# Experts with the gate on each expert's output, and another order of work in the selective scan and the last attention

## The chip, the cores and the metric

The kernel runs on one core of a Trainium2 chip. A core has TensorE (PE, matrix products into PSUM), VectorE (DVE), ScalarE (ACT), GpSimd (POOL) and SyncE (SP), which runs no arithmetic here. Each engine works through its own list of instructions in order, and they wait for one another by semaphores. The metric is the device time of the whole program in microseconds. The numbers of the text are microseconds where no unit stands.

## The reference, cut to what matters

Eight sublayers on 2048 tokens of 128 features, each followed by an addition and a LayerNorm. The change touches the second (`L0_ffn`), the fifth (`L2_attn`) and the seventh (`L3_attn`), and the LayerNorm behind them.

```python
x = layernorm(x + L0_ffn(x))     # and so on for the eight sublayers

def L0_ffn(x):                   # 8 experts, hidden 512, the best 2 of each token count
    logits = x @ router_w.T + router_b
    topk_val, topk_idx = top_k(logits, 2)
    weights = softmax(topk_val)
    outs = [silu(x @ w1a.T + b1a) * (x @ w1b.T + b1b) @ w2.T + b2 for each expert]
    return sum over the two chosen of outs[idx] * weight

def L2_attn(x):
    xs, z = split(x @ W_in)      # 128 channels each; both: silu(depthwise conv, 4 taps)
    dt_low, Bc, Cc = split(xs @ W_xdbl)        # 64, 16, 16
    delta = softplus(dt_low @ W_dt + 2 * inv_dt)
    # for each of 16 states n and each token l of 4 sequences of 256:
    h = exp(-(n + 1) * delta) * h + delta * xs * Bc[n]
    y = sum over n of h * Cc[n]  + xs * D
    return concat(y, silu(z)) @ W_out + b_out

def L3_attn(x):                  # 16 heads, 4 key/value heads of 64
    return softmax(q @ k.T) @ v @ o_w.T + o_b
```

## The kernel before, in words

Features or channels lie on the 128 partitions and tokens along the free axis in *blocks* of 512 (4 blocks, 16 *tiles* of 128 tokens). For LayerNorm the tokens lie on the partitions (`X`, 16 tiles). Each sublayer is a class with one method for each engine (`pe`, `act`, `dve`, `pool`) that issues that engine's instructions in program order; a counter such as `hid` or `gated` is a semaphore, and `e.wait_ge(*self.hid(j))` waits for its j-th step. There is no planner: the order written in these methods is the order of the work. No DMA stands in the loops that the change touches.

*Experts* (`Experts`, line 585). The loop has 128 jobs i: block b = i // 32, expert x = i // 4 % 8, and one quarter kb = i % 4 of the hidden features. For a job, PE does six f16 matmuls of 512 columns (`first`: the operands are split into a high and a low f16 part, L680 to L682) into two banks; ACT takes silu of the first bank into `S1` (L770); POOL multiplies it by the gate row of the expert, spread over the partitions, `GS` (L881); DVE adds the bias to the second bank and multiplies (L820, into `HF`, the gated product); ACT rounds that to f16 (L776); DVE takes the remainder, the low part (L814); PE does three down matmuls (L723 to L725), three jobs behind. All 32 jobs of a block add up in one bank (6 or 7), which begins with the gated second bias (`MB2` by the gates `GT`). `GS` is made by PE (L709, a spread of the gates by a constant matrix) and ACT at the first job of each expert. On DVE the order within an iteration is: low part of job i−2, gated product of job i−1, and up to iteration 24 a pair of instructions for the low parts of the next weights (`w_low`, L801). At the end of a block ACT copies the bank to SBUF, PE transposes it (L730) and DVE does the LayerNorm's addition and statistics (L305, L312, L315) before it goes on with the next product. The scaling of all 16 tiles follows after the last block. Before the loop, DVE picks the experts and computes the gates (`gates`), and PE and ACT transpose and copy them.

*Selective scan* (`Mamba`, line 1295). 32 *units* u: a half of the tokens (1024, two blocks b = 0, 1) by 16 states n. For a unit PE spreads the row B for both blocks (`rows_b`, L1460) and the row C for both (`rows_c`, L1468, both into bank 6, so the second waits for ACT's copy of the first, L1595) and adds up the unit before (`add_up`, two fp32 matmuls, L1478). ACT makes the decay of unit u + 2 (`decay_of`, L1588). DVE scales the input (`scale_in`, two instructions), and does the scan (`dve_scan`, L1689). POOL multiplies the result by the C row (L1718). Parts 2 and 3 of the projections, the delta of the second half and the second convolution (`pe_gate`) are distributed over units 1 to 31 by the `if u ==` chains in `pe`, `act`, `dve` and `pool`. `dve_y` (L1694) finishes the first half's output.

*Last attention* (`Attention`, line 2314). 32 pairs ji, each of 16 groups g: PE's scores, DVE's row maxima (L2743), with which PE continues (L2497), ACT's exponentials (L2638), sums on DVE (L2761) and POOL (L2813). After every eighth pair DVE adds the block (`dve_add`, g = 7 of ji % 8 = 0), and in the pair behind takes the statistics (g = `STATS` = 0) and the scale factors with the scaling of 4 tiles (g = `SCALE` = 2); ACT scales the other half of these tiles. `LayerNorm(k, 1)` scales block by block; `LayerNorm(k)` scales once, after all four.

## Time and profile before

| | |
|---|---|
| time, median of 3 runs | 2797.37 (2792.01 to 2798.61) |
| the profiled execution's own time | 2786.94 |
| its span | 2784.8 |
| mean granted TensorE clock (share of full speed) | 0.959 |
| PE, DVE, ACT, POOL busy (page) | 88%, 73%, 52%, 43% |

The busy shares are means over eleven stages that follow one another. The times in the timelines count from the span's start. In them, several like instructions in a row are put together (x2), and "[0.76 <-ACT WK L776]" says that the engine had been idle for 0.76 us and that ACT's instruction of line 776 ended this. Experts' first layers (L680) start from 110 to 418, the scans (L1689) from 675 to 813, and the last attention's row maxima (L2743) from 1407 to 2582.

### The profile page before, as it was taken

The numbers are of one execution on the slowest core, as the hardware profiler recorded it, in microseconds if no ns is written. First come the engines' busy times: TensorE is split into PE (matmuls) and PEld (weight loads), VectorE is DVE, ScalarE is ACT, GpSimd is POOL, SyncE is SP. The second block draws the span as 40 slices with busy tenths as digits, with TensorE's granted clock in tenths as the row PEclk, the third lists the DMA queues.
The fourth block names the chain that finished last, engine by engine and source line by source line (L and its number), as shares of the span: only waits on it lengthen the run. The fifth ranks groups of instructions, "written<-read, shape, count | busy, mean of one in ns | idle before, by whom it ended". The sixth has DMA issues, their size and how long they took to land.

```text
span 2784.8 us, 40142 instructions
## 1 busy us (share of the span) xinstructions
PE 2443.4 (88%) x14918; PEld 1121.1 (40%) x14918; DVE 2040.9 (73%) x3152; ACT 1440.9 (52%) x2509; POOL 1185.3 (43%) x748
## 2 busy tenths in 40 slices
PE   6689995797777987798679999999999999999897
PEld 4434332444234665466423333333333333333344
DVE  7686666616888984897578888788878888788542
ACT  5465552534646773576235555455545555455462
POOL 1155550402645541554105555445545555455530
PEclk9799997898998999999889999999999999999999
DMA  5000000101000000000010000000000000000000
GB/s 205 1 1 1 1 1 0 54 1 42 1 1 16 1 1 1 1 1 2 16 42 5 9 9 9 9 7 7 9 9 9 9 9 9 5 9 9 9 1 16
DMA packets 20831, 37.92 MB, mean 14 GB/s; under 512 B 10462, under 2 KB 12638, under 8 KB 19612
## 3 DMA queue, kind: packets, MB, share of 16 engines
q1 hardware_dynamic: 20636, 35.35, 3.7%
q8 instruction: 119, 1.95, 0.3%
q14 instruction: 76, 0.62, 0.1%
HBM read 32.99 MB, written 2.35 MB: 13 GB/s over the span
## 4 chain that ended last, share of the span: by engine, by line
PE 56%; DVE 30%; issue 7%; ACT 5%; POOL 1%; DMA 0%; ACTq 0%; DVEq 0%; POOLq 0%; SPq 0%
PE PS L2536 12%; PE PS L2527 12%; PE PS L1184 6%; DVE NR L2743 5%; PE PS L2497 5%; DVE W L2761 2%; DVE WK L820 2%; DVE NR L270 2%; DVE WK L2075 2%; PE PS L1478 2%; PE PS L1166 2%; DVE WK L2051 2%; DVE WK L267 1%; ACT WK L776 1%; PE PS L2483 1%
## 5 line engine op out<-in xcount | busy, mean ns | idle before, releaser
L2743 DVE TENSOR_REDUCE NR<-PS 128x2 f32<-128x1024 f32 x512 | 626.1, 1223 | 208.5 <-PE PS L2498 208.4
L2638 ACT ACTIVATE WK<-PS 128x1024 f32<-128x1024 f32 x512 | 496.9, 1022 | 488.9 <-PE PS L2527 416.5
L2813 POOL TENSOR_TENSOR W<-W,WK 128x1024 f32<-128x1024 f32 x224 | 527.2, 2354 | 482.0 <-DVE W L2761 413.0
L2536 PE MATMUL PS<-WK,W 128*64 128x512 f32 x2048 | 494.1, 603 | 0.0
L2527 PE MATMUL PS<-WK 64*128 64x512 f16 (+1 forms) x4096 | 485.5, 377 | 0.0
L2761 DVE TENSOR_TENSOR W<-W,WK 128x1024 f32<-128x1024 f32 x224 | 284.9, 1272 | 14.4 <-ACT WK L2638 14.3
L2527 PEld LDWEIGHTS PS<-WK 64*128 64x128 f16 (+1 forms) x4096 | 199.3, 94 | 220.1 <-ACT WK L2638 6.5
L881 POOL TENSOR_TENSOR WK<-WK 128x512 f32<-128x512 f32 x128 | 168.0, 1313 | 154.0 <-ACT WK L770 154.0
L2497 PE MATMUL PS<-WK 64*128 64x512 f16 x512 | 196.4, 384 | 36.9 <-DVE NR L2743 34.7
L2536 PEld LDWEIGHTS PS<-WK,W 128*64 128x64 f32 x2048 | 124.1, 136 | 249.3 <-issue 174.3
L2498 PE MATMUL PS<-WK 64*128 64x512 f16 x512 | 196.4, 384 | 0.0
L1184 PE MATMUL PS<-WK,W 128*128 128x512 f16 x768 | 166.1, 379 | 0.0
L2497 PEld LDWEIGHTS PS<-WK 64*128 64x128 f16 x512 | 47.8, 93 | 285.9 <-DVE NR L2743 227.7
L814 DVE TENSOR_TENSOR WK<-WK 128x512 f16<-128x512 f32 x128 | 96.9, 757 | 77.0 <-ACT WK L776 77.0
L2098 POOL TENSOR_TENSOR WK<-WK 128x512 f32<-128x512 f32 x64 | 113.4, 1793 | 93.9 <-DVE WK L2035 93.7
L1988 ACT ACTIVATE WK<-PS,WK 128x192 f32<-128x192 f32 (+1 forms) x256 | 103.7, 428 | 89.8 <-DVE WK L2075 89.7
L776 ACT ACTIVATE WK<-WK 128x512 f16<-128x512 f32 x128 | 80.6, 630 | 107.9 <-DVE WK L820 107.8
L2106 POOL TENSOR_TENSOR WK<-WK 128x768 f32<-128x768 f32 (+1 forms) x64 | 91.5, 1448 | 101.9 <-DVE WK L2028 101.9
L1184 PEld LDWEIGHTS PS<-WK,W 128*128 128x128 f16 x768 | 75.1, 98 | 90.6
L820 DVE SCALAR_TENSOR_TENSOR WK<-PS,WK 128x512 f32<-128x512 f32 x128 | 95.0, 742 | 8.9 <-POOL WK L881 8.9
L680 PE MATMUL PS<-WK 128*128 128x512 f16 x256 | 99.5, 389 | 1.6 <-ACT WK L770 1.6
L1718 POOL TENSOR_TENSOR WK<-WK 128x512 f32<-128x512 f32 x64 | 80.0, 1271 | 47.4 <-ACT WK L1595 42.2
(364 smaller groups left out, 4343.4 us busy)
## 6 DMA issues: line engine op xcount, KB each, us to landing
XB<-l_rdens SPq DMA_DIRECT2D x62, 128.0 KB, 2.9
W<-in_mw SPq DMA_DIRECT2D x8, 512.0 KB, 12.2
W<-in_l2w SPq DMA_DIRECT2D x1, 3114.0 KB, 12.2
W<-in_f1w SPq DMA_DIRECT2D x1, 2816.0 KB, 18.7
W<-in_l3w SPq DMA_DIRECT2D x1, 2816.0 KB, 10.3
W<-in_f3w SPq DMA_DIRECT2D x1, 2816.0 KB, 9.8
W<-in_mw SPq DMA_DIRECT2D x8, 256.0 KB, 12.2
CBB<-in_cbb SPq DMA_DIRECT2D x1, 1360.0 KB, 8.3
```

The source lines that it names most:

```text
L820: e.scalar_tensor_tensor(out=self.HF[j % 3], in0=k.bank(2 + j % 3), scalar=self.MB1[:, x * 8 + 4 + kb:x * 8 + 5 + kb], in1=self.S1[j % 3], ...
L881: e.tensor_tensor(s1, s1, self.GS[i // 4 % 2], ALU.mult).then_inc(self.gated.sem)
L1184: i = e.matmul(k.bank(2 + (n + 2) % 6), wp[p][:, kb, o], src[q][:, kb, s_], start=kb == 0 and j == 0, stop=kb == 3 and j == 2)
L2098: e.tensor_tensor(p5[:, :, :, hf, :], q5[:, :, :, 1 - hf, :], self.SN[:, t, :, hf * 32:hf * 32 + 32].unsqueeze(2).broadcast_to([P, 2, 8, 3 ...
L2497: e.matmul(k.bank(6), q[0:64, ts_], self.KH[0:64, g, ks], start=True, stop=True)
L2498: e.matmul(k.bank(7), q[64:128, ts_], self.KH[64:128, g, ks], start=True, stop=True).then_inc(self.maxs.sem)
L2527: m = e.matmul(k.bank(2 * (kt % 2) + i), keys[own, :], queries[own, :], start=j == 0, stop=j == 3)
L2536: m = e.matmul(k.PS[64 * i:64 * i + 64, 4, :], self.V[:, kt, g, :], self.PTB[kt // 2 % 2][:, kt % 2, i, :], start=kt == 0, stop=kt == NT - 1)
L2638: e.activation(self.PTB[kt // 2 % 2][:, kt % 2, :, :], self.k.PS[:, 2 * (kt % 2):2 * (kt % 2) + 2, :], ACT.Exp, scale=1.0 / 64).then_inc(s ...
L2743: e.tensor_reduce(self.PM[ji % 2][:, u // 4, :, u % 4], self.k.PS[:, 6:8, :], AX.X, ALU.max).then_inc(self.maxes.sem)
L2761: e.tensor_tensor(ac, ac, p, ALU.add).then_inc(self.acc0.sem)
L2813: e.tensor_tensor(ac, ac, p, ALU.add).then_inc(self.acc1.sem)
```

## The change

*Experts.* silu is no longer multiplied by the gate. DVE's product writes in place into `S1` (four buffers instead of three), the low part is a scalar_tensor_tensor that scales by 0.125, and each expert has a bank of its own, 6 + n % 2 with n the number of block and expert. When an expert's four down products are in, DVE multiplies the bank by the gate row into `TM` (the first expert of a block: into the sum `ACC`), and POOL adds `TM` to `ACC`. The second bias is added in `pe_rows`, where PE multiplies by the gates `GT` and turns the sum, seven jobs after the block's end; `dve_rows` does addition and statistics at iterations 41, 73, 105 and at the end. The gate's spread is now at the third job of each expert; the transposes of the gates (`pe_gates`, `act_gates`) are inside the loop at i = 2, and four parts of the low weights stand around `gates`.

*Scan.* Adding up half 0 of the unit before is put between the two C rows. The pieces for parts 2 and 3 move by a unit or more on PE and ACT, and `dve_y` from unit 16 to 17.

*Last attention.* The statistics are taken in two halves at g = 4 of the two pairs behind a block; the scaling is done once, after the last block, for 16 tiles.

The diff, cut to its core:

```diff
-    def dve_stats(self, e, b):
-        k = self.k
+    def dve_stats(self, e, b, part=0, parts=1):
+
+        k, n = self.k, 4 // parts
         xs = k.X[:, 4 * b:4 * b + 4, :]
         e.wait_ge(*self.added(b + 1))
-        for j in range(4):
+        for j in range(n * part, n * part + n):
             e.bn_stats(k.ST[:, b, j, :], xs[:, j, :]).then_inc(self.stats.sem)
-        e.wait_ge(*self.stats(8 * b + 4))
-        for j in range(4):
+        e.wait_ge(*self.stats(8 * b + 2 * n * part + n))
+        for j in range(n * part, n * part + n):
             e.bn_aggr(k.MV[:, b, j, :], k.ST[:, b, j, :]).then_inc(self.stats.sem)
...
-        self.S1 = [wk(16384 + i * 512, 512) for i in range(3)]
-        self.HF = [wk(17920 + i * 512, 512) for i in range(3)]
...
+        self.S1 = [wk(16384 + i * 512, 512) for i in range(4)]
+        self.HP = [wk(18432 + i * 512, 512).bitcast(F16).rearrange("p (s n) -> p s n", s=2) for i in range(4)]
+        self.TM = wk(20480, 512)
+        self.ACC = [k.XB[:, :, :].rearrange("p t f -> p (t f)"), wk(20992, 512)]
+        self.MB1 = wk(21504, 64)
...
+        for i in range(128 + 3):
+            if i < 128:
+                b, x, kb = self.job(i)
+                if kb == 2:
+                    if i == 2:
+                        self.pe_gates(e)
+                    else:
+                        e.wait_ge(*self.gs(i // 4))
+                    if x == 2 and b:
+                        e.wait_ge(*self.ln.added(b))
+                    e.matmul(k.bank(5), k.cb("selm", x * 128, (x + 1) * 128, p1=96), self.G3[0:96, b * 512:(b + 1) * 512], start=True, stop=True).then_inc(self.gbc.sem)
+                if i > 1:
+                    first(i)
+                if x == 1 and kb == 3 and b:
+                    self.pe_rows(e, b - 1)
+            if i >= 3:
+                b, x, kb = self.job(i - 3)
+                n = (i - 3) // 4
+                hb, acc = self.HP[(i - 3) % 4], k.bank(6 + n % 2)
+                q = slice(1024 + kb * 128, 1024 + (kb + 1) * 128)
+                if not kb and n >= 2:
+                    e.wait_ge(*self.gated(n - 1))
+                if n < 2 and not kb:
+                    e.wait_ge(*self.gt(8))
+                e.wait_ge(*self.hl(i - 2))
+                e.matmul(acc, self.WH[x][:, q], hb[:, 0, :], start=not kb, stop=False)
+                e.matmul(acc, self.WL[x][:, q], hb[:, 0, :], start=False, stop=False)
+                e.matmul(acc, self.WH[x][:, q], hb[:, 1, :], start=False, stop=kb == 3).then_inc(self.down.sem)
+        self.pe_rows(e, 3)
...
+    def pe_rows(self, e, b):
+
+        k, PS = self.k, self.k.PS
+        e.wait_ge(*self.gs(8 * b + 10 if b < 3 else 32))
+        e.wait_ge(*self.summed(7 * b + 7))
+        for j in range(4):
+            o, t = PS[:, 5, j * 128:(j + 1) * 128], 4 * b + j
+            e.matmul(o, self.GT[0:8, t * 128:(t + 1) * 128], k.c("mb2", p1=8), start=True, stop=False)
+            i = e.matmul(o, self.ACC[b % 2][:, j * 128:(j + 1) * 128], k.eye, start=False, stop=True)
+        i.then_inc(self.otr.sem)
...
-                if x == 7 and kb == 3:
-                    e.wait_ge(*self.gs(8 * (b + 1) + (b < 3)))
-                    e.wait_ge(*self.out(b + 1))
-                    for q in range(4):
-                        i_ = e.transpose(PS[:, 5, q * 128:(q + 1) * 128], k.XB[:, q, :], k.eye)
-                    i_.then_inc(self.otr.sem)
...
+        for i in range(128 + 1):
+            if i == 2:
+                self.act_gates(e)
+            if i < 128:
+                b, x, kb = self.job(i)
+                if kb == 3:
+                    n = i // 4
+                    if n >= 2:
+                        e.wait_ge(*self.gated(n - 1))
+                    e.wait_ge(*self.gbc(n + 1))
+                    e.activation(self.GS[n % 2], k.bank(5), ACT.Copy, scale=1.0 / 64).then_inc(self.gs.sem)
+                if i >= 4:
+                    e.wait_ge(*self.hl(i - 3))
+                e.wait_ge(*self.up(2 * i + 1))
+                e.activation(self.S1[i % 4], k.bank(i % 2), ACT.Silu, bias=c("mb1", x * 8 + kb, x * 8 + kb + 1), scale=1.0 / 64).then_inc(self.silu.sem)
+            if 1 <= i:
+                j = i - 1
+                if j >= 4:
+                    e.wait_ge(*self.down(j - 3))
+                e.wait_ge(*self.hid(j + 1))
+                e.activation(self.HP[j % 4][:, 0, :], self.S1[j % 4], ACT.Copy, scale=0.125).then_inc(self.hh.sem)
...
-                    e.activation(k.XB[:, :, :].rearrange("p t f -> p (t f)"), k.bank(6 + b % 2), ACT.Copy, scale=1.0 / 512).then_inc(self.out.sem)
-                    self.ln.act(e, b)
...
-        e.tensor_scalar(self.MB2[0:8, :], c("mb2", p1=8), 512.0, None, ALU.mult).then_inc(self.bias.sem)
+        w_low(1, 0)
+        w_low(1, 1)
         self.gates(e)
-        for n in range(4, 4 + self.AHEAD):
-            w_low(n // 4, n % 4)
-        for i in range(128 + 3):
+        w_low(1, 2)
+        w_low(1, 3)
+        e.wait_ge(*self.bias(1))
+        for i in range(128 + 4):
             if 2 <= i < 130:
                 j = i - 2
                 hb = self.HP[j % 4]
                 e.wait_ge(*self.hh(j + 1))
-                e.tensor_tensor(hb[:, 1, :], self.HF[j % 3], hb[:, 0, :], ALU.subtract).then_inc(self.hl.sem)
+                e.scalar_tensor_tensor(out=hb[:, 1, :], in0=self.S1[j % 4], scalar=0.125, in1=hb[:, 0, :], op0=ALU.mult, op1=ALU.subtract).then_inc(self.hl.sem)
             if 1 <= i < 129:
                 j = i - 1
                 b, x, kb = self.job(j)
                 e.wait_ge(*self.up(2 * j + 2))
-                e.wait_ge(*self.gated(j + 1))
-                e.scalar_tensor_tensor(out=self.HF[j % 3], in0=k.bank(2 + j % 3), scalar=self.MB1[:, x * 8 + 4 + kb:x * 8 + 5 + kb], in1=self.S1[j % 3], op0=ALU.add, op1=ALU.mult).then_inc(self.hid.sem)
+                e.wait_ge(*self.silu(j + 1))
+                e.scalar_tensor_tensor(out=self.S1[j % 4], in0=k.bank(2 + j % 3), scalar=self.MB1[:, x * 8 + 4 + kb:x * 8 + 5 + kb], in1=self.S1[j % 4], op0=ALU.add, op1=ALU.mult).then_inc(self.hid.sem)
...
+            if i >= 7 and i % 4 == 3:
+                self.dve_gate(e, i // 4 - 1)
+            if i > 32 and i % 32 == 9:
+                self.dve_rows(e, i // 32 - 1)
+        self.dve_rows(e, 3)
+
+    def dve_gate(self, e, n):
+
+        b, x = n // 8, n % 8
+        if not x:
+            if b >= 2:
+                e.wait_ge(*self.otr(b - 1))
+        elif n > 1:
+            e.wait_ge(*self.summed(7 * b + x - 1))
+        e.wait_ge(*self.gs(n + 1))
+        e.wait_ge(*self.down(4 * n + 4))
+        e.tensor_tensor(self.TM if x else self.ACC[b % 2], self.k.bank(6 + n % 2), self.GS[n % 2], ALU.mult).then_inc(self.gated.sem)
+
+    def dve_rows(self, e, b):
+        e.wait_ge(*self.otr(b + 1))
+        self.ln.dve(e, b, four(self.k.PS[:, 5, :]))
...
-        for i in range(128):
-            s1 = self.S1[i % 3]
-            if i % 4 == 0:
-                e.wait_ge(*self.gs(i // 4 + 1))
-            e.wait_ge(*self.silu(i + 1))
-            e.tensor_tensor(s1, s1, self.GS[i // 4 % 2], ALU.mult).then_inc(self.gated.sem)
+        for n in range(32):
+            b, x = n // 8, n % 8
+            if x:
+                acc = self.ACC[b % 2]
+                if x > 1:
+                    e.wait_ge(*self.summed(7 * b + x - 1))
+                e.wait_ge(*self.gated(n + 1))
+                e.tensor_tensor(acc, acc, self.TM, ALU.add).then_inc(self.summed.sem)
...
                 self.rows_b(e, u + 1, 0)
                 self.rows_b(e, u + 1, 1)
             self.rows_c(e, u, 0)
+            if u:
+                self.add_up(e, u - 1, 0)
             self.rows_c(e, u, 1)
             if u:
-                self.add_up(e, u - 1, 0)
                 self.add_up(e, u - 1, 1)
             if u == 1:
                 self.pe_low(e, 2)
-            elif u == 3:
+            elif u == 4:
                 self.pe_low(e, 3)
-            elif u == 5:
+            elif u == 6:
                 self.pe_dt(e, 2)
-            elif u == 7:
+            elif u == 8:
                 self.pe_dt(e, 3)
             elif self.Z0 <= u < self.Z0 + 16:
                 self.pe_gate(e, u - self.Z0)
...
             if u == 2:
                 self.act_low(e, 2)
             elif u == 4:
+                self.act_mid(e, 2)
+            elif u == 5:
                 self.act_low(e, 3)
-            elif u == 5:
-                self.act_mid(e, 2)
             elif u == 6:
+                self.act_mid(e, 3)
+            elif u == 7:
                 self.act_abs(e, 2)
                 self.act_pos(e, 2)
-            elif u == 7:
-                self.act_mid(e, 3)
-            elif u == 8:
+            elif u == 9:
                 self.act_abs(e, 3)
                 self.act_pos(e, 3)
-            elif u == 9:
+            elif u == 10:
                 self.act_exp(e, 1)
-            elif u == 10:
+            elif u == 11:
                 self.act_ln(e, 2)
                 self.act_ln(e, 3)
             elif u >= self.Z0 + 4 and (u - self.Z0) % 4 == 0 and u <= self.Z0 + 16:
...
                 self.dve_rem(e, 2)
             elif u == 5:
                 self.dve_rem(e, 3)
-            elif u == 16:
+            elif u == 17:
                 self.dve_y(e, 0)
                 self.dve_y(e, 1)
         e.wait_ge(*self.biased(1))
...
     PROJECT, AHEAD = 4, 5
     TOP, ROW, LOW = 4, 6, 6
     SUM, INVERT, MULTIPLY, PRODUCT = 1, 3, 4, 7
-    STATS, SCALE = 0, 2
+    STATS = 4
 
     def __init__(self, k, ld, const, rows):
         self.k, self.ld, self.const = k, ld, const
...
         self.rwide = k.counter("l3_reciprocals_wide", 31 * 32)
         self.ot = k.counter("l3_divided", 32)
         self.prod = k.counter("l3_products", 4)
-        self.ln = LayerNorm(k, 1)
+        self.ln = LayerNorm(k)
 
 
 
...
                     self.act_output(e, ji - 1)
                 if g == self.SUM and ji:
                     self.act_denominators(e, ji - 1)
-                if g == self.SCALE + 1 and ji > 8 and ji % 8 == 1:
-                    self.ln.act(e, ji // 8 - 1)
         self.act_output(e, 31)
         self.ln.act(e, 3)
 
...
                 if g == self.PRODUCT and ji and ji % 8 == 0:
                     e.wait_ge(*self.prod(ji // 8))
                     self.ln.dve_add(e, ji // 8 - 1, four(k.PS[:, 5, :]))
-                if g == self.STATS and ji > 8 and ji % 8 == 1:
-                    self.ln.dve_stats(e, ji // 8 - 1)
-                if g == self.SCALE and ji > 8 and ji % 8 == 1:
-                    self.ln.dve_scale(e, ji // 8 - 1)
+                if g == self.STATS and ji > 8 and 1 <= ji % 8 <= 2:
+                    self.ln.dve_stats(e, ji // 8 - 1, ji % 8 - 1, 2)
         self.dve_sum(e, 31, 7)
         self.dve_join(e, 31)
         self.dve_last_invert(e)
```

## Rows read from the trace of the kernel before

**Rows 1.** The page: busy time of each engine, and the chain that ended last.
```profile
PE 2443.4 (88%) x14918; PEld 1121.1 (40%) x14918; DVE 2040.9 (73%) x3152; ACT 1440.9 (52%) x2509; POOL 1185.3 (43%) x748
...
PE 56%; DVE 30%; issue 7%; ACT 5%; POOL 1%; DMA 0%; ACTq 0%; DVEq 0%; POOLq 0%; SPq 0%
```

**Rows 2.** Timeline, Experts loop: start us, us, engine line op [idle before <-releaser].
```profile
302.12 0.74 DVE L820 SCALAR_TENSOR_TENSOR WK<-PS,WK 128x512 f32<-128x512 f32 x1
303.62 0.69 DVE L814 TENSOR_TENSOR WK<-WK 128x512 f16<-128x512 f32 x1 [0.76 <-ACT WK L776]
304.22 0.75 DVE L820 SCALAR_TENSOR_TENSOR WK<-PS,WK 128x512 f32<-128x512 f32 x1
...
306.08 0.68 ACT L770 ACTIVATE WK<-PS,CB 128x512 f32<-128x512 f32 x1
...
306.90 1.27 POOL L881 TENSOR_TENSOR WK<-WK 128x512 f32<-128x512 f32 x1 [1.39 <-ACT WK L770]
...
307.83 0.88 DVE L814 TENSOR_TENSOR WK<-WK 128x512 f16<-128x512 f32 x1 [0.76 <-ACT WK L776]
...
308.78 0.39 PE L723 MATMUL PS<-WK 128*128 128x512 f16 x1 [0.19 <-DVE WK L814]
```

**Rows 3.** Timelines of DVE and PE, start and end of Experts.
```profile
133.96 0.74 DVE L820 SCALAR_TENSOR_TENSOR WK<-PS,WK 128x512 f32<-128x512 f32 x1
...
422.71 0.74 DVE L820 SCALAR_TENSOR_TENSOR WK<-PS,WK 128x512 f32<-128x512 f32 x1
...
427.13 1.09 PE L730 MATMUL PS<-CB,XB 128*128 128x128 f32 x4 [0.78 <-ACT XB L786]
```

**Rows 4.** Timelines of DVE and POOL, where both start close together.
```profile
146.83 1.70 DVE L801 SCALAR_TENSOR_TENSOR WK<-W,WK 128x256 f16<-128x256 f32 x2
147.11 1.27 POOL L881 TENSOR_TENSOR WK<-WK 128x512 f32<-128x512 f32 x1 [1.95 <-ACT WK L770]
...
156.82 0.61 DVE L801 SCALAR_TENSOR_TENSOR WK<-W,WK 128x256 f16<-128x256 f32 x2
157.11 1.44 POOL L881 TENSOR_TENSOR WK<-WK 128x512 f32<-128x512 f32 x1 [1.97 <-ACT WK L770]
...
2584.85 2.35 POOL L2813 TENSOR_TENSOR W<-W,WK 128x1024 f32<-128x1024 f32 x1 [1.16 <-DVE W L2761]
2584.87 3.40 DVE L2761 TENSOR_TENSOR W<-W,WK 128x1024 f32<-128x1024 f32 x1
```

**Rows 5.** Timeline of DVE, the end of block 0 of Experts.
```profile
208.36 0.74 DVE L820 SCALAR_TENSOR_TENSOR WK<-PS,WK 128x512 f32<-128x512 f32 x1
...
211.58 0.69 DVE L305 TENSOR_TENSOR X<-PS,X 128x512 f32<-128x512 f32 x1 [2.48 <-PE PS L730]
...
214.09 0.74 DVE L820 SCALAR_TENSOR_TENSOR WK<-PS,WK 128x512 f32<-128x512 f32 x1
```

**Rows 6.** One line's view, the scans: min/median/max ns, first and last start us.
```profile
L1689 DVE TENSOR_TENSOR_SCAN WK<-WK,PS x16: 2286/2287/2289, 675.2 to 744.0; 128x1024 f32<-128x1024 f32 x16
...
L1689 DVE TENSOR_TENSOR_SCAN WK<-WK,NR,PS x16: 2347/2347/2349, 748.4 to 812.8; 128x1024 f32<-128x1024 f32 x16
```

**Rows 7.** Timelines of PE and DVE in the scan.
```profile
720.48 0.60 PE L1460 MATMUL PS<-WK,CBB 96*128 96x512 bf16 x2
...
722.05 0.39 PE L1468 MATMUL PS<-WK,CBB 96*128 96x512 bf16 x1 [0.76 <-ACT WK L1595]
...
724.86 0.60 PE L1460 MATMUL PS<-WK,CBB 96*128 96x512 bf16 x2
...
753.70 1.61 DVE L1694 SCALAR_TENSOR_TENSOR WK<-WK,CB,PS 128x512 f32<-128x512 f32 x2 [2.92 <-PE PS L1478]
```

**Rows 8.** Timelines of DVE and PE in the last attention.
```profile
1798.24 0.16 DVE L323 TENSOR_SCALAR NR<-MV 128x4 f32<-128x4 f32 x1
...
1801.21 1.22 DVE L2761 TENSOR_TENSOR W<-W,WK 128x1024 f32<-128x1024 f32 x1
...
1803.62 0.39 PE L2497 MATMUL PS<-WK 64*128 64x512 f16 x1 [2.75 <-DVE NR L2743]
```

More of the change, by code:

```diff
@@ L751, in act, with act_gates @@
         e.activation(self.GW[:, 1, :], self.GW[:, 0, :], ACT.Exp).then_inc(self.gexp.sem)
+        for i in range(128 + 1):
[19 more added lines that the diff above has]
+                e.activation(self.HP[j % 4][:, 0, :], self.S1[j % 4], ACT.Copy, scale=0.125).then_inc(self.hh.sem)
+            n = i + 4 + self.AHEAD
+            if n < 32:
+                w_high(n // 4, n % 4)
+        for b in range(NB):
+            self.ln.act(e, b)
+    def act_gates(self, e):
+        k = self.k
         for b in range(NB):
@@ L757, in act @@
             e.activation(self.G3[0:96, s_], k.bank(7, p1=96), ACT.Copy).then_inc(self.gt.sem)
-        for i in range(128 + 3):
-            if i < 128:
-                b, x, kb = self.job(i)
-                if not kb:
-                    n = i // 4
-                    if n >= 2:
-                        e.wait_ge(*self.gated(4 * (n - 1)))
-                    e.wait_ge(*self.gbc(n + 1))
-                    e.activation(self.GS[n % 2], k.bank(5), ACT.Copy).then_inc(self.gs.sem)
-                if i >= 3:
-                    e.wait_ge(*self.hid(i - 2))
-                e.wait_ge(*self.up(2 * i + 1))
-                e.activation(self.S1[i % 3], k.bank(i % 2), ACT.Silu, bias=c("mb1", x * 8 + kb, x * 8 + kb + 1), scale=1.0 / 64).then_inc(self.silu.sem)
-            if 1 <= i < 129:
-                j = i - 1
-                if j >= 4:
-                    e.wait_ge(*self.down(j - 3))
-                e.wait_ge(*self.hid(j + 1))
-                e.activation(self.HP[j % 4][:, 0, :], self.HF[j % 3], ACT.Copy).then_inc(self.hh.sem)
-            n = i + 4 + self.AHEAD
-            if n < 32:
-                w_high(n // 4, n % 4)
-            if i >= 3:
-                b, x, kb = self.job(i - 3)
-                if x == 7 and kb == 3:
-                    e.wait_ge(*self.down(32 * (b + 1)))
-                    if b:
-                        e.wait_ge(*self.otr(b))
-                    e.activation(k.XB[:, :, :].rearrange("p t f -> p (t f)"), k.bank(6 + b % 2), ACT.Copy, scale=1.0 / 512).then_inc(self.out.sem)
-                    self.ln.act(e, b)
     def dve(self, e):
@@ L823, in dve @@
                 w_low(n // 4, n % 4)
-            if i >= 3:
-                b, x, kb = self.job(i - 3)
-                if x == 7 and kb == 3:
-                    e.wait_ge(*self.otr(b + 1))
-                    self.ln.dve(e, b, four(PS[:, 5, :]))
+            if i >= 7 and i % 4 == 3:
[16 more added lines that the diff above has]
+        self.ln.dve(e, b, four(self.k.PS[:, 5, :]))
     def gates(self, e):
```

52 lines of the change are left out of this document (11 added, 41 removed).

## The prediction

> **What bounds the kernel now.** I read the page first. TensorE (PE) is busy 88% of the span and has 56% of the chain that ended last, but DVE has 30% of it [rows 1], so the limit changes from stage to stage, and I went on stage by stage with the timelines.
>
> In the Experts loop the order on DVE is: low part of job j, gated product of job j+1, and so on. The product (L820) starts at 302.12; ACT rounds it; the low part (L814) starts at 303.62, after 0.76 of idle time that ACT's L776 ended; the next product starts at 304.22 [rows 2]. This is a ring, DVE to ACT to DVE, of 2.10 to 2.11 us for a job, and PE needs less: nine matmuls at 0.216 from start to start are 1.94, with a quarter of the gate's spread 2.0, and it does idle for DVE's low part (0.19 before 308.78 [rows 2]). GpSimd (POOL), busy 1.27 in every job, is not in the ring except at each expert's first job: its multiply starts late (306.90), and the low part takes 0.88 in place of 0.69 [rows 2]. 308.71 (its end) is 0.54 after POOL's end at 308.17: the low part did not run slower, it waited. So four jobs take 8.63 (4 times 2.11 and 0.19).
>
> In the scan (u = 0 to 31), DVE alone would need 1.29 for two input scalings, less an overlap, and 2.29 or 2.35 for the scan itself, 3.72 or 3.81 a unit; the starts of the 32 scans go from 675.2 to 812.8 [rows 6], 137.6 for 31 intervals, where DVE alone needs about 119. The rest is PE. Its cycle in the units with a gate convolution is 4.37 (720.48 to 724.86) [rows 7], and 0.76 of it is a wait for ACT's copy between the two C rows. In the last attention, PE and DVE hand the row maxima to and fro, and a stretch of other work on DVE stops PE: during the 2.97 from 1798.24 to 1801.21 and after it PE sat idle for 2.75 [rows 8].
>
> **The change, part by part.**
>
> *Experts, ring.* POOL's 128 multiplies of 1.27 go. The low part becomes a scalar_tensor_tensor with the same shapes; I take 0.69 (the types are the same, and the ring's other operand is unchanged). The rounding on ACT keeps its size, so the ring stays 2.11. Added on DVE: 32 products of bank and gate, PSUM against SBUF, 128x512; the LayerNorm's addition has that shape and took 0.69 [rows 5]. It is put right after a gated product, in the 0.76 in which DVE idles, so it costs nothing there. In the first block the slot also holds the low weights (a pair takes 0.61 undisturbed [rows 4]); five gates fall there, about 0.3 each, and four POOL additions delay the next pair by 0.2 each: 2.4.
>
> *Experts, POOL's 28 additions.* This is the term that decides. Each reads two SBUF operands, 1.27 as the multiplies of that shape, and starts when the gate product ends. A gate product starts 0.66 after the gated product L820, ends 0.60 after that one's end, thus at about 1.35; POOL starts 0.14 after what it waits for in the two-signal form (ACT's end 306.76 to 306.90 [rows 2]): 1.49. The low part starts at 1.50. A tie within 0.02. The loser waits for the winner's whole instruction: if POOL wins, the low part ends 0.54 after POOL, at 3.30 and not at 2.19, 1.06 to 1.1 later, in the ring; if DVE wins, POOL waits and nobody minds. Nearest rows: DVE starting 0.02 after POOL lost (3.40 for an instruction of 1.22 [rows 4]). Two pairs of DVE instructions, whose second starts 0.33 after the first: with POOL 0.28 behind the first it lost (1.70 for the pair), with POOL 0.29 behind it won (0.61, POOL 1.44) [rows 4]. So there DVE still wins when it starts about 0.04 after POOL; an instruction that starts from idle needs some 0.015 more, which puts the edge near 0.025, just where the lost case lies. I expect the low part 0.01 after POOL, so DVE wins, by a hair. Bounds: 0 and 1.06 for each of the 23 additions that lie in the ring outside the low weights' time. Three of them (second expert of blocks 1 to 3) wait for one signal only, so POOL is earlier and wins: 3.2. I take the other 20 at 0.
>
> The Trainium skill ("SBUF — State Buffer", the section on the engine ports) says that VectorE with two SBUF inputs and GpSimd share a port pair under an exclusive lock, and that whichever starts first has it for the whole instruction while the other fully blocks. The blocking agrees with the trace (0.88, 3.40). By its "starts first", POOL would win all 23; that is the first rival below. The pair of 0.61 shows a later start that won.
>
> *Experts, block ends.* Before: from product to product 5.73 (208.36 to 214.09) in place of 2.11, of which 2.48 is the wait for PE's transposes [rows 5]; 3.62 too much, three times. After: PE turns the sums four to seven jobs later. It waits for the gate row that ACT copies, does eight fp32 matmuls of 128 columns (about 2.1 at the slower clock, as the four transposes took 1.09 [rows 3]), and its next first layer is late for ACT by about 2.1, of which the ring feels 1.1; then DVE's addition and statistics, 1.93, stand where 0.76 was idle, 1.1 more. 2.2, and 2.7 with PE at the lower clock in part. From the third gated product (133.96) to the last (422.71) the kernel took 288.75 [rows 3]. After: 125 rings of 2.11 are 263.75, and 2.4, 3.2 and 8.1 make 277.4: minus 11.3.
>
> *Experts, ends.* The gates' transposes and copies (about 5.3) now come after the first gated product, not before it, and silu's table is loaded while DVE picks the experts. I place the third product at 129.6, not 133.96 [rows 3]: minus 4 (3 to 5). At the end, after the last down matmul: gate product 0.69, POOL 1.27, eight matmuls, where there were a copy of 0.6 and four transposes: plus 2.4 where the transposes end, at 428.22 [rows 3]. Experts: minus 12.9.
>
> *Scan.* Adding up half 0 before the second C row puts 0.86 of matmuls into the 0.76 wait. PE's cycle becomes 3.5 with the convolution, under DVE's 3.81. The old excess over DVE alone: 0.55 to 0.6 in each of eight units, 4.6; PE's backlog at units 6 and 8 1.3; the log's two table loads, after which a decay on ACT is late for DVE, and the backlog behind, 5.1; the outputs of the first half, 2.92 until PE's additions [rows 7], now a unit later when they are done; the start, 3.5, of which the new order takes 1.7. Sum 15.6, and half a microsecond behind the last scan. The remainders for channel part 3 are now taken by ACT and DVE in the same unit: DVE waits about 1.0. I forecast minus 14 (8 to 16), as some table-load stall may remain.
>
> *Last attention.* Three scale chains leave DVE: 2.97 each, 2.85 of it felt [rows 8]: minus 8.6. The statistics go from one 1.2 in group 0 to twice 0.6 in group 4, where DVE idles for PE's row matmuls but PE waits for the next maximum: plus 0.3, three times. The last scaling covers 16 tiles, not 4: ACT does eight of 0.4 in place of two, less transposes that follow behind: plus 1.8 (up to 2.3). Sum minus 5.9.
>
> Total: 12.9, 14 and 5.9 are 32.8. From the profiled execution's 2786.94, that gives 2754.1; the median of the three runs is 2797.37, 0.37% above it, so 2764.5, say **2765 us**.
>
> **The rivals.**
>
> *POOL wins every tie.* For: it is the plain order of starts, and the 0.02 case. Against: the pair at 0.61. Price 20 times 1.06, 21.2 more: 2786. A mixture lies between.
>
> *The scan gains half.* The table loads stall DVE as before and the late remainders cost more; with DVE winning the ties, 7 less: 2772.
>
> *PE stops in the new place (slower).* Half 0's addition stands before the second C row and so before ACT's copy and POOL's next product. If POOL's product of half 0 is not ready when PE gets there (it has about 0.4 to spare by my count), PE, ACT and POOL wait in a chain. From 0.4 of lateness on it decides; at one product's 1.27 a unit, less 0.4, 31 units lose 27 and the scan's 14 are gone: 2765 + 41, about 2806. Against: POOL idles a third of the unit.
>
> *The late transposes do not shorten the Experts* (block ends as before, plus the longer end): 2765 + 3: it stays in the first case's range.
>
> **How the numbers follow.** DVE wins 0.50 (own range 2756 to 2775); POOL wins 0.28; scan gains half 0.10; small mishaps of both kinds 0.08; PE stops 0.04. About 0.3% (8 us) is what a measurement of this kernel tells from no change. Faster by more than it is below 2789: nearly all of the first and third cases and four fifths of the second, whose 2786 lies 3 under that limit: 0.88 with half of the mishaps. Same 0.08, slower 0.04. The range reaches to the POOL case: 2753 to 2791.
>
> **What would show it.** In the profile after: the low part (128x512, f16 out) near 0.69 in each job, and 1.7 to 1.8 in three or in 23 of them, says who wins; product to product 2.11 between. Gate products must not be ended by a wait for PE. Block ends near 4.8, not 5.73. The scans' starts should span about 123, without 4.37 intervals; a wait of DVE for ACT's remainder of about 1.0 appears once. In the last attention no PE gap of 2.75. The prediction is wrong if the ring's period is not 2.11, if low parts wait elsewhere, or if scan intervals stay above 3.9.

## The result

The changed kernel is slower by 0.3%: 2803.72 (median of 16 runs, 2794.98 to 2806.08) against 2793.49 before (16 runs, 2788.43 to 2798.61), ratio 1.0032 (95% interval 1.0024 to 1.0041), where the prediction said 2765 and a range of 2753 to 2791. The profiled execution of before (2786.94) was quicker than any of the sixteen, that of after (2803.48) an average one, so the two traces differ by 16.5 where the medians differ by 10.2.

The page after: engines' busy time, and the chain, beside [rows 1].

```profile
PE 2468.4 (88%) x14958; PEld 1142.8 (41%) x14958; DVE 2059.4 (74%) x3144; ACT 1438.3 (51%) x2505; POOL 1055.0 (38%) x648
...
PE 53%; DVE 30%; issue 9%; ACT 6%; POOL 1%; DMA 0%; ACTq 0%; DVEq 0%; POOLq 0%; SPq 0%
```

POOL (GpSimd) is busy 130 less and DVE (VectorE) 18.5 more, although DVE executes eight instructions fewer. To see where, I took for each stage the time from PE's first matrix product in it to that of the next stage (the first attention and the last feed-forward, which are left out, differ by 0.1 and 1.1):

| stage | before | after |
|---|---|---|
| Experts | 340.0 | 361.2 |
| decay attention | 86.1 | 90.5 |
| ternary feed-forward | 130.4 | 132.1 |
| selective scan | 187.5 | 180.4 |
| local attention and its feed-forward, two layers | 556.5 | 557.9 |
| last attention | 1251.7 | 1246.1 |

Scan and last attention gain, 7.1 and 5.6. Experts was to give 12.9 and takes 21.2 more. The groups of DVE's instructions in the changed kernel, from 110 to 460 (busy us, mean ns | idle before them):

```profile
L825 DVE SCALAR_TENSOR_TENSOR WK<-WK 128x512 f16<-128x512 f32 x128 | 113.4, 886 | 84.6 <-ACT WK L782 84.6
L831 DVE SCALAR_TENSOR_TENSOR WK<-PS,WK 128x512 f32<-128x512 f32 x128 | 95.1, 743 | 0.0
L851 DVE TENSOR_TENSOR WK<-PS,WK 128x512 f32<-128x512 f32 x30 | 20.4, 680 | 1.7 <-PE PS L712 1.7
```

The low part (L825) has a mean of 886 ns. Its median is 692 ns; 23 of the 128 take 1.52 to 1.80 us, the others at most 0.70. The timelines of DVE and of POOL about two of the 23, beside the ring of [rows 2]:

```profile
306.45 0.68 DVE L851 TENSOR_TENSOR WK<-PS,WK 128x512 f32<-128x512 f32 x1
307.29 1.73 DVE L825 SCALAR_TENSOR_TENSOR WK<-WK 128x512 f16<-128x512 f32 x1 [0.16 <-ACT WK L782]
308.94 0.74 DVE L831 SCALAR_TENSOR_TENSOR WK<-PS,WK 128x512 f32<-128x512 f32 x1
...
316.76 1.80 DVE L825 SCALAR_TENSOR_TENSOR WK<-WK 128x512 f16<-128x512 f32 x1 [0.16 <-ACT WK L782]
```

```profile
307.21 1.26 POOL L910 TENSOR_TENSOR XB<-XB,WK 128x512 f32<-128x512 f32 x1 [21.08 <-DVE WK L851]
...
316.75 1.26 POOL L910 TENSOR_TENSOR XB<-XB,WK 128x512 f32<-128x512 f32 x1 [8.28 <-DVE WK L851]
```

In 19 of the 23 (such as that of 316.76), POOL's addition starts 0.013 to 0.017 before the low part, and the low part takes 1.80: it ends 0.55 after POOL's end, where it was 0.54 in [rows 2]. In the other four POOL is further ahead: 0.08 at the first addition of blocks 1 to 3 (such as that of 307.29), and 0.29 at the second of block 1. The 23 together are 25.0 too long.

The second cost is the block end, where PE turns the block's sum so that the tokens lie on the partitions. PE's timeline about i = 39 (x2 is two instructions), PE's window over the turning (stretch, length, busy, PEclk, DMA share, GB/s), and the low part that is late behind it:

```profile
210.73 0.61 PE L739 MATMUL PS<-CB,XT 8*128 8x128 f32 x2 [1.81 <-ACT WK L772]
211.27 0.80 PE L740 MATMUL PS<-CB,XB 128*128 128x128 f32 x2
212.00 0.79 PE L739 MATMUL PS<-CB,XT 8*128 8x128 f32 x2
...
215.62 0.80 PE L740 MATMUL PS<-CB,XB 128*128 128x128 f32 x2
```

```profile
210.73:216.40 5.67, 5.67 (x17) 0.52 0.00 0
```

```profile
220.31 0.69 DVE L825 SCALAR_TENSOR_TENSOR WK<-WK 128x512 f16<-128x512 f32 x1 [6.62 <-ACT WK L782]
```

Each fp32 product is two instructions on PE (L739 and L740 have 32 each, where the code issues 16), and after 1.81 of idle time PE runs them at the lower clock (granted 0.52 over the window): 16 instructions, 5.5 from the first at 210.73 to what follows them, and PE's next first layers start 0.43 apart and not 0.22. The interval from gated product to gated product is 7.97 there, 5.49 and 6.38 at the next two block ends, and in each case about 3.2 right behind, where DVE's addition and statistics stand. The granted clock of the stretch about these three ends is the lower one for 10.2, 3.4 and 6.8. The end of Experts, in the timelines of PE and DVE:

```profile
443.41 0.77 PE L739 MATMUL PS<-CB,XT 8*128 8x128 f32 x2 [2.38 <-POOL WK L910]
...
448.44 0.80 PE L740 MATMUL PS<-CB,WK 128*128 128x128 f32 x2
```

```profile
449.28 0.69 DVE L305 TENSOR_TENSOR X<-PS,X 128x512 f32<-128x512 f32 x1 [7.42 <-PE PS L740]
```

From the last gated product (437.33) to this addition 11.95, where it was 5.55 before (422.71 [rows 3], addition at 428.26).

The scan, one line's view as in [rows 6]: from the first to the last start 127.1 in place of 137.6.

```profile
L1719 DVE TENSOR_TENSOR_SCAN WK<-WK,PS x16: 2286/2287/2289, 703.9 to 768.2; 128x1024 f32<-128x1024 f32 x16
L1719 DVE TENSOR_TENSOR_SCAN WK<-WK,NR,PS x16: 2346/2347/2347, 772.8 to 831.1; 128x1024 f32<-128x1024 f32 x16
```

In the last attention no gap of 2.75 is left; the pair of heads that held it takes 44.0 in place of 46.9 to 48.6, three times, and the scaling at the end has eight activations in a row on ACT:

```profile
2655.51 3.19 ACT L341 ACTIVATE X<-X,NR 128x128 f32<-128x128 f32 x8 [17.40 <-DVE NR L327]
```

### The profile page after: what moved, and what is told of

It is laid out like the page before. It is cut to its first block, busy times and chain, and to the rows that moved or that the text cites. A ratio compares the mean times of both kernels' runs of the same rounds, so it can differ in the third digit from the quotient of the medians.

```text
span 2801.7 us, 40162 instructions
## 1 busy us (share of the span) xinstructions
PE 2468.4 (88%) x14958; PEld 1142.8 (41%) x14958; DVE 2059.4 (74%) x3144; ACT 1438.3 (51%) x2505; POOL 1055.0 (38%) x648
## 4 chain that ended last, share of the span: by engine, by line
PE 53%; DVE 30%; issue 9%; ACT 6%; POOL 1%; DMA 0%; ACTq 0%; DVEq 0%; POOLq 0%; SPq 0%
PE PS L2566 13%; PE PS L2557 12%; PE PS L1213 6%; DVE NR L2769 5%; PE PS L2527 5%; DVE WK L831 3%; DVE W L2787 2%; DVE NR L270 2%; DVE WK L2105 2%; PE PS L1195 2%; DVE WK L2081 1%; ACT WK L782 1%; DVE WK L267 1%; DVE WK L2088 1%; PE PS L2513 1%
## 5 line engine op out<-in xcount | busy, mean ns | idle before, releaser
L825 DVE SCALAR_TENSOR_TENSOR WK<-WK 128x512 f16<-128x512 f32 x128 | 113.4, 886 | 84.6 <-ACT WK L782 84.6
L2128 POOL TENSOR_TENSOR WK<-WK 128x512 f32<-128x512 f32 x64 | 113.4, 1792 | 94.1 <-DVE WK L2065 93.9
L776 ACT ACTIVATE WK<-PS,CB 128x512 f32<-128x512 f32 x128 | 86.3, 674 | 27.5 <-PE PS L682 27.0
L680 PE MATMUL PS<-WK 128*128 128x512 f16 x256 | 99.7, 389 | 0.1
L682 PE MATMUL PS<-WK 128*128 128x512 f16 x256 | 99.6, 389 | 0.0
L681 PE MATMUL PS<-WK 128*128 128x512 f16 x256 | 99.6, 389 | 0.0
## 6 DMA issues: line engine op xcount, KB each, us to landing
W<-in_f3w SPq DMA_DIRECT2D x1, 2816.0 KB, 10.2
```

Source lines behind the costliest of these rows:

```text
L825: e.scalar_tensor_tensor(out=hb[:, 1, :], in0=self.S1[j % 4], scalar=0.125, in1=hb[:, 0, :], op0=ALU.mult, op1=ALU.subtract).then_inc(self ...
L2128: e.tensor_tensor(p5[:, :, :, hf, :], q5[:, :, :, 1 - hf, :], self.SN[:, t, :, hf * 32:hf * 32 + 32].unsqueeze(2).broadcast_to([P, 2, 8, 3 ...
```

## The experiments

Each kernel's ratio is its time over that of the kernel before on the same chip; scan_only and attn_only ran 11 times, the others four or five times. The first three take the change apart.

**exp_only, scan_only, attn_only**: the kernel before with the hunks of one of the three parts.

> Only the Experts part of the change. Theory A (the loss is in Experts: 23 low parts that wait for POOL at 1.1 each, block ends that grew from 3.6 to about 6 extra, a longer end, less 10 at the start): 20 to 26 us slower than before, ratio 1.007 to 1.009; the low parts of 1.8 are there again. Rival B (the pieces disturb one another, Experts alone costs little): under 10 us slower.

> Only the scan's new order. Theory A: 7 to 11 us faster (the scans' starts span about 127 in place of 137.6). Rival B: the whole 14 of my prediction, which after's profile hid by a lower clock at its end; then the scans span 123 to 125. Rival C: within 3 us, the gain in the profile came from the clock.

> Only the last attention's part (statistics in two halves, scaling once at the end). Theory A: 5.6 us faster, ratio 0.998, the last attention shorter by that and no other stage changed. Rival B: no difference.

Measured: Experts alone 1.0090 (1.0076 to 1.0104), 2816.10 against 2791.69; scan alone 0.9979 (0.9970 to 0.9988), 2785.43; attention alone 0.9979 (0.9970 to 0.9988), 2785.28. In us against 2791.69: +24.4, −6.3, −6.4, together +11.7, and the whole change has +10.2: within the intervals the parts add. The scan's 6.3 is a little under the 7 to 11 expected. The loss lies in Experts, whose stage takes 361.0 alone and 361.2 in the whole; the low parts of 1.8 are there again, at the same 23 places.

**pool_late**: is it POOL?

```diff
                 e.wait_ge(*self.gated(n + 1))
+                e.wait_ge(*self.hl(min(4 * n + 7, 128)))
                 e.tensor_tensor(acc, acc, self.TM, ALU.add).then_inc(self.summed.sem)
```

> The changed kernel, where POOL's addition of an expert's gated output waits in addition for the low part that it met before (of job 4n+6, at most the last), so that it starts when that one has ended. Theory A (the port: POOL starts 0.01 before DVE and DVE waits for its whole instruction): all low parts at 0.69, 23 x 1.1 = 25 us less than the changed kernel, thus about 15 us faster than before, ratio 0.995. Rival B (the low part of 1.8 is slow for another reason, such as the gate product right before it): no change from the changed kernel, ratio 1.003. Rival C: POOL now meets the next low part, 2.1 later, and costs the same again.

Measured: 0.9942 (0.9929 to 0.9956), 2776.77. Not one low part is over 0.70. From the third gated product to the last it is 284.7 and not 307.5. The gate product stands where it stood, so it wasn't that (rival B), and the next low part isn't met (rival C).

**pool_hh**: how near may two starts be?

```diff
                 e.wait_ge(*self.gated(n + 1))
+                e.wait_ge(*self.hh(min(4 * n + 7, 128)))
```

> The changed kernel, where POOL's addition waits in addition for ACT's rounding of the same job, the very instruction that releases DVE's low part; so both are released together and POOL starts some hundredths behind DVE instead of 0.015 before it. Theory A (who starts first has the port, to the hundredth): DVE wins all, low parts 0.69, POOL's addition stretched to 1.6 or so, 25 us less than the changed kernel, ratio about 0.995. Rival B (a start within some 0.05 is decided for POOL, or at random): low parts of 1.8 in all or some, between 0.995 and 1.003.

Measured: 0.9937 (0.9916 to 0.9958), 2774.14. DVE and POOL of this kernel, at such a job:

```profile
311.41 0.69 DVE L825 SCALAR_TENSOR_TENSOR WK<-WK 128x512 f16<-128x512 f32 x1 [0.16 <-ACT WK L782]
```

```profile
311.54 1.68 POOL L911 TENSOR_TENSOR XB<-XB,WK 128x512 f32<-128x512 f32 x1 [6.75 <-ACT WK L782]
```

POOL now starts 0.11 to 0.14 behind the low part and is the one that waits, 1.68 in place of 1.26, where nobody needs it. Against 0.015 ahead, a shift of 0.15 is worth 26 us. From third to last it is 281.1, where pool_late had 284.7: 1.5 of that is in the first block, where pool_late's additions meet the low weights' pairs, and 2.1 at the block ends (5.64, 6.05 and 6.81 for 6.30, 7.48 and 6.60). At the first two the lower clock lasts 3.4 in place of 6.8; no run shows what sets that.

**pl_bias, pl_later, pl_all**: what does a block end cost? All have pool_late's wait. pl_bias adds the second bias, which PE has put into a column for each expert, in DVE's gate product, and PE only transposes the sum:

```diff
-        e.tensor_tensor(self.TM if x else self.ACC[b % 2], self.k.bank(6 + n % 2), self.GS[n % 2], ALU.mult)...
+        e.scalar_tensor_tensor(out=self.TM if x else self.ACC[b % 2], in0=self.k.bank(6 + n % 2), scalar=self.MB2C[:, x:x + 1], in1=self.GS[n % 2], op0=ALU.add, op1=ALU.mult)...
...
-            e.matmul(o, self.GT[0:8, t * 128:(t + 1) * 128], k.c("mb2", p1=8), start=True, stop=False)
-            i = e.matmul(o, self.ACC[b % 2][:, j * 128:(j + 1) * 128], k.eye, start=False, stop=True)
+            i = e.transpose(PS[:, 5, j * 128:(j + 1) * 128], self.ACC[b % 2][:, j * 128:(j + 1) * 128], k.eye)
```

pl_later keeps the products and turns the sum one job later (i = 40):

```diff
-                if x == 1 and kb == 3 and b:
+                if x == 2 and kb == 0 and b:
                     self.pe_rows(e, b - 1)
```

pl_all has both, and DVE's block work in pieces:

```diff
             if i > 32 and i % 32 == 9:
-                self.dve_rows(e, i // 32 - 1)
+                e.wait_ge(*self.otr(i // 32))
+                self.ln.dve_add(e, i // 32 - 1, four(self.k.PS[:, 5, :]))
+            if i > 32 and i % 32 in (10, 12):
+                self.ln.dve_stats(e, i // 32 - 1, i % 32 // 2 - 5, 2)
```

> The kernel with POOL's addition behind the low part; besides, the second bias is added as a column in DVE's gate product (scalar_tensor_tensor for tensor_tensor, 0.74 for 0.69), so that PE turns the sum with 4 transposes in place of 8 fp32 matrix products. Theory A (my prediction took the fp32 products at the price of transposes; they cost 3.3 at the full clock and 5.8 at the lower, transposes 0.5 to 1.1): 2 to 3 less at each of three block ends and 4.5 less at the end, 10 to 14 us less than the kernel with POOL behind (2777), thus about 2765. Rival B (the block ends cost what they cost by PE's wait for the gate row, and the product is hidden in it): 5 less, the end alone.

> The kernel with POOL's addition behind the low part; besides, PE turns the sum one job later (behind the first layer of i = 40 instead of 39). The wait of 1.8 for ACT's copy of the gate row, which ACT can't start before the job's order lets it, is over by then. Theory A (PE's wait costs, and lets the clock drop behind it): 1.5 to 3 less at each block end, 5 to 9 us less than 2777. Rival B (the 8 products alone exhaust the ring's slack, the wait is off the path): under 2 less.

> All of it: POOL behind the low part, the bias in the gate product with 4 transposes, these one job later, and DVE's block statistics in halves at iterations 10 and 12 instead of all at 9 (each piece at most 0.69 beside 0.76 of idle time). Theory A: block ends cost under 1 in place of 5.8, 15 less for the three, 4.5 less at the end: about 2757. Rival B: the pieces do not add, since the ring has one slack only: 2765.

Measured: pl_bias 0.9887 (0.9868 to 0.9905), 2761.22; pl_later 0.9895 (0.9877 to 0.9913), 2763.61; pl_all 0.9862 (0.9839 to 0.9884), 2757.23. PE's timelines at the first block end and (408.63) the end of pl_bias, then at the first block end of pl_later:

```profile
211.54 0.66 PE L740 MATMUL PS<-CB,XB 128*128 128x128 f32 x4 [1.81 <-ACT WK L772]
...
408.63 1.09 PE L740 MATMUL PS<-CB,WK 128*128 128x128 f32 x4 [2.43 <-POOL WK L913]
```

```profile
208.90 0.48 PE L739 MATMUL PS<-CB,XT 8*128 8x128 f32 x2
...
211.81 0.49 PE L740 MATMUL PS<-CB,XB 128*128 128x128 f32 x2
```

Both expectations put the gain at the block ends too low, and the traces show why. Either edit alone removes the whole long interval (6.30, 7.48 and 6.60 in pool_late; none over 3.2 in pl_bias or pl_later): PE has slack for the wait of 1.81 (pl_bias) or for 3.3 of products at the full clock (pl_later), and in neither is the clock low at a block end. With both it drops each time, and the longer it stays low the longer the interval: 3.4 of lower clock with 5.45 to 6.05, 6.8 with 6.30 to 7.48, 10.2 with 7.86 and 7.97 (twelve block ends of after, exp_only, pool_late and pool_hh). From third to last it is 271.1 and 270.7. pl_bias gains 5.3 more at the end of the stage (6.6 from the last gated product to the addition, for 11.9 in pl_later), and loses 1.3 at its start, where DVE waits 2.67 for the transposed bias before it goes on with the weights, and pl_later 1.40 for PE; so the two come out near each other (the stages 320.7 and 324.5). The pieces of pl_all take off the 3.2 intervals in two of three blocks; in the first there are two long ones (3.18 and 2.80), and from third to last it is 270.5. Its Experts stage, 321.1, is no shorter than pl_bias's 320.7, and the intervals of the two ratios overlap: that the pieces add anything to the bias column isn't shown, and its block ends came under the 1 expected in two blocks only.

**addup_only**: what gives the scan's gain?

```diff
             self.rows_c(e, u, 0)
+            if u:
+                self.add_up(e, u - 1, 0)
             self.rows_c(e, u, 1)
             if u:
-                self.add_up(e, u - 1, 0)
                 self.add_up(e, u - 1, 1)
```

> The kernel before with one edit of the scan: half 0 of the unit before is added up between the two C rows; all other pieces stay at their units. Theory A (this edit takes the 0.76 wait off PE, and with it the 4.37 intervals of the units with a gate convolution): the intervals of 4.37 become 3.81, the scans span 4 to 6 less than 137.6, the kernel 4 to 6 us faster. Rival B (the gain of the scan's part comes from the pieces that move by a unit): under 2 us.

Measured: 0.9953 (0.9939 to 0.9967), 2780.33 against 2792.79, 12.5 less and twice what scan_only had; in the stage it is 10.0 less (177.5), where scan_only had 6.8. The whole scan part does worse than one of its edits, and theory A (4 to 6) had half of the size. The scans start from 677.7 to 802.7, 125.0. The intervals of 4.36 at 15 and from 23 to 27 are 3.75 and 3.81, 3.4 together; most of the rest is at 3 (7.22 to 4.61), at 12 and 13 (5.85 and 6.79 to 4.65 and 5.18) and at 17 (8.21 to 5.84).

**best, best_rem, best_noln, best2**: best is the changed kernel with pool_hh's wait, pl_all's edits, and the two small instructions of the bias column later on DVE. best_rem moves one remainder:

```diff
-            elif u == 5:
+            elif u == 6:
                 self.dve_rem(e, 3)
```

with ACT's `act_mid(3)` at 7 and `act_abs(2)`, `act_pos(2)` at 6. best_noln has in best the line

```diff
-        ... ACT.Ln, bias=...
+        ... ACT.Exp if b >= 2 else ACT.Ln, bias=...
```

and best2 is best with all pieces for parts 2 and 3 at the units they had before, on PE and ACT; only the addition between the C rows and `dve_y` at 17 are kept.

> The changed kernel with POOL released by ACT's rounding, the bias column (its two small instructions late enough not to hold DVE at the start), the transposes one job later and the statistics in halves. Theory A (each was a cost of its own): the kernel with all but the first and last of these took 2757; 3.6 less in block 0 and 2.6 less at the start: 2751, ratio 0.984. Rival B (they share what they give): 2757.

> The one before, with the remainder of channel part 3 taken by DVE at unit 6 instead of 5 (ACT's following step at 7 instead of 6). Theory A (DVE waits 1.43 for ACT's copy at unit 5, and PE's clock drops behind that idle time): the interval of 5.9 between scans 5 and 6 becomes 4.5, 1.5 to 3 us less than the one before. Rival B (PE's delta product waits for the same remainder, so the wait moves to PE at unit 6): no difference.

> The combination kernel (best) with the logarithm of the second half's softplus replaced by an exponential, so that ACT loads no other table in the scan; this leaves the logarithm of half the tokens out, its time only is of use. Theory A (the two table loads cost DVE 1.3 at unit 13 and, by PE's idle time and its lower clock, 2.7 at unit 14): the two intervals of 5.1 and 6.4 become 3.75 each plus at most half a us, 3.5 to 4.5 us less than the combination. Rival B (a unit takes as long without, since ACT has to do the two logarithms anyway): under 1.5 less.

> The combination kernel (best) with the scan's pieces for parts 2 and 3 put back to their old units on PE and ACT; the addition of half 0 between the C rows stays, and so do the outputs at unit 17. Theory A (the moved pieces cost, the addition alone gives the gain): the scans span 124 to 124.5 in place of 127.15, the stage from its first matrix product to the next stage takes 176.5 in place of 180.4, 3.5 less than the combination's 2755.8: about 2752. Rival B (the moved pieces do no harm, addup_only was short for another reason): the stage stays at 180.

| | ratio (interval) | us | scans | scan stage |
|---|---|---|---|---|
| best | 0.9871 (0.9856 to 0.9886) | 2755.78 | 127.2 | 180.4 |
| best_rem | 0.9856 (0.9841 to 0.9871) | 2754.35 | 123.9 | 177.1 |
| best_noln | 0.9849 (0.9834 to 0.9865) | 2751.70 | 121.9 | 173.9 |
| best2 | 0.9858 (0.9841 to 0.9876) | 2750.75 | 122.6 | 174.7 |

The whole times lie within one another's intervals; the stage times tell them apart (the scan stage is 180.3 to 180.7 in all eight traces that have the whole scan part). Experts takes 318.6 in best, 21.4 less than before and 42.6 less than after. But best as a whole isn't measurably quicker than pl_all, so of its theory's 6 only the stage's 2.5 stands. best_rem: the interval of 5.87 before scan 6 becomes 3.75 and the next, 3.75 before, 4.46: theory A, with 1.4. The stage has 3.3 less; another 1.8 is at the table loads (5.11 and 6.43 become 4.44 and 5.34), where PE's clock is low for 3.4 in place of 6.8. Whether the moved remainder did that, no run shows. best_noln: the two intervals at the table loads, 5.11 and 6.43, become 3.75 each, and the next two 3.75 and 3.81 for 4.23 and 4.52; 5.2 in the scans, 6.5 in the stage, more than expected. Its log of half the tokens is left out, so it is no version to use. best2, its scans as above:

```profile
L1725 DVE TENSOR_TENSOR_SCAN WK<-WK,PS x16: 2286/2287/2289, 659.8 to 719.4; 128x1024 f32<-128x1024 f32 x16
L1725 DVE TENSOR_TENSOR_SCAN WK<-WK,NR,PS x16: 2346/2347/2348, 724.1 to 782.4; 128x1024 f32<-128x1024 f32 x16
```

Theory A of best2 holds, by more than it said (174.7, expected 176.5). best2 has the lowest median here, 1.4% under the kernel before, but its ratio can't be told from those of pl_all and best_rem.

## Why the prediction was wrong, point by point

**Experts, the ring: right.** In pool_late all intervals outside the block ends and the low weights' time are 2.11 but one (2.38), and the low part in its new form takes 0.69. The 32 gate products cost nothing in the ring.

**Experts, POOL's additions: this is the step that failed.** The tie was foreseen to a few thousandths (the low part 0.01 after POOL; measured 0.013 to 0.017), but I let DVE win it, on the strength of one pair that won from 0.04 behind [rows 4], and against the row 2584.87, which lost from 0.02. All 19 ties lost, and the four with POOL further ahead as well: 25.0 where the sum had 3.2. The pair was an exception. In all fifteen traces 16 DVE instructions with two SBUF inputs ended before the POOL instruction that had started before them, each the second of such a pair and 0.034 to 0.046 behind; every one that started from idle, from 0.013 behind on, ended behind it. The pair's second instruction had been queued behind a running one of its engine and the low part starts from idle, which may be the reason, but it isn't shown: in pl_bias a queued addition that started 0.031 behind POOL lost too (2187.88, 2.32). The Trainium skill ("SBUF — State Buffer", the section on the engine ports) says that whichever starts first gets the port pair for the whole instruction. The trace agrees at 0.015 in one direction and at 0.135 in the other (pool_hh). My first rival was this; with its 21 the sum would have been 2786, still 18 under the measured time.

**Experts, block ends: mis-sized.** 2.7 each stood in the sum. In pool_late, where POOL is out of it, they cost 5.5, 6.4 and 5.5 over the ring, 17.4 for 8.1. I priced a fp32 product like one of the four transposes of [rows 3] (1.09 for the four). A product is two instructions, 0.72 together at that clock: eight are 5.8 and not 2.1. The trace of the kernel before shows it (L1478 is there 128 times for 64 additions). I had seen PE's wait for the gate row, but not that it lets the clock drop. pl_bias and pl_later show both halves: with either gone the block end costs 1.05, DVE's own work, as forecast.

**Experts, start: right** (third product at 129.82, forecast 129.6). **End: mis-sized** for the same reason, 6.4 and not 2.4; pl_bias takes 5.3 off it. With the measured terms the stage's sum is −4.1, +18.7 and +6.4, that is 21.0 of the 21.2.

**Scan: the mechanism was right, 14 was 6 to 7.** The second C row was the limit of PE, and the 4.36 intervals are gone but where the table loads stand. But I counted the moved pieces as gain. addup_only and best2 show that they are a loss: DVE waits 1.43 for ACT's copy at unit 5 (its remainder stood "about 1.0" in the sum, once), PE is idle for 2.42 behind it, and falls to the lower clock. The changed kernel's timeline of DVE:

```profile
727.83 0.69 DVE L1674 TENSOR_TENSOR WK<-PS,WK 32x512 f32<-32x512 f32 x1 [1.43 <-ACT WK L1584]
...
757.57 2.29 DVE L1719 TENSOR_TENSOR_SCAN WK<-WK,PS 128x1024 f32<-128x1024 f32 x1 [1.49 <-ACT WK L1618]
...
762.57 1.29 DVE L1708 TENSOR_TENSOR PS<-W,PS 128x512 f32<-128x512 f32 x2 [2.72 <-PE PS L1490]
```

The last two rows are the table loads, which I had as gone (5.1) and which stay, 4.0 in the two intervals they stand in and 5.2 by best_noln. And behind the last scan the output's products ran at the lower clock, so that the first addition followed 9.25 after the scan's start and not 8.14.

**Last attention: right.** 5.9 was forecast, 5.6 is the stage's difference and 6.4 that of the medians. One trace is not the size to the last us: without the edit the stage took 1251.7, 1253.8, 1253.9 and 1257.2 in four traces, with it 1243.2 to 1246.8 in eleven, so the gain may be nearer 8. The pair right behind a block takes 3 to 4.6 less, the next one 0.6 more (1.1 once), and ACT's scaling at the end is the longer one forecast.

**Slower than before:** no rival's mechanism alone did it. It took the first rival (+21.8), two terms whose price I had not doubted (block ends +9.3, end +4.0) and half of the scan's gain (+7). These 42 lift my −32.8 to about +9, near the 10.2 between the medians; the rest of the traces' 16.5 is the stages with no edit, 4.4 of it in the decay attention. The rival of PE stopping in the scan had named 2806, near the measured time, but by chance: the scans' starts span 127.1, and nothing of its chain is there. I had bounded POOL's term from both sides, but not that of the fp32 products, the one new operation in the change whose nearest row was of another kind.

## What to carry to other kernels

When two engines that block each other are released within a tenth of a us, don't argue who wins: look which start comes first, take the loss in full, and fix the order with a wait on the off-path engine. It cost one line and was worth 26 us. Price an operation by rows of the same operation, counting the instructions that the trace shows for each one issued. Where several reorderings come as a package, run each by itself: here the package of the scan held an edit worth 12.5 and moved pieces that cost 5.7 in the stage (best against best2).

## What the runs showed of the hardware

- POOL's start 0.013 ahead of DVE's was enough to block it for 1.1. In no trace here did a DVE instruction from idle win from behind.
- Fp32 transposes of 128x128 started 0.21 apart at the lower clock and 0.11 at the full one (raw starts of L730 and of pl_bias's L740); fp32 products of that size 0.72 and 0.42, on the average of 8. The Trainium skill ("TensorE: Matmul & The Clock Gate", the table of terms) gives the transpose mode a factor of 4 for fp32; these starts show 3.4 and 3.8.
- The same decay attention, in code that nobody touched, took 84.8 to 90.5 from one profiled execution to another, and the more of it PE spent at the lower clock, the longer it took, but for one trace: 34.9 to 38.7 of lower clock with 86.1 to 86.5, 43.1 with 87.5, 45.6 to 48.8 with 88.8, 56.4 with 90.5 (the one is best, 37.0 with 84.8). In the changed kernel's trace PE's granted clock was low for most of it; windows of PE, the changed kernel first, then the one before (columns: stretch, length, busy, PEclk, DMA share, GB/s):

```profile
471.00:496.00 25.00, 14.11 (x33) 0.64 0.00 0
496.00:516.00 20.00, 12.11 (x40) 0.59 0.00 0
```

```profile
450.00:475.00 25.00, 13.03 (x36) 0.75 0.00 1
475.00:490.00 15.00, 6.59 (x36) 1.00 0.00 1
```

  0.5 is 1.2 GHz and 1.0 is 2.4 GHz. A few us of a difference between two traces can come with this alone: exp_only, with the same Experts, had 86.5 there.
